# GpSimd's weight and condition splits in 256-column instructions, and the first down-weight split moved ahead of a wait

## What is computed

```python
h = _gcn(h, src, dst, gcn_in_w, gcn_in_b, n)
for i in range(L):                                   # L = 4
    a = _attn(_ln(h, ln2_w[i], ln2_b[i]), cond, Wq[i], Wk[i], Wv[i], Wo[i])
    h = h + a
    u = _ln(h, ln3_w[i], ln3_b[i]) @ geglu_w[i] + geglu_b[i]
    val, gate = jnp.split(u, 2, axis=-1)
    f = val * jax.nn.gelu(gate, approximate=False)
    h = h + f @ ffo_w[i] + ffo_b[i]
h = _gcn(h, src, dst, gcn_out_w, gcn_out_b, n)
```

## Time and profile before

| | us |
|---|---|
| median of 3 runs | 2378.5 (2378.1 to 2378.63) |
| the profiled execution, whole | 2377.68 |
| its span in the trace | 2375.9 |
| TensorE busy | 2315.6 |
| VectorE busy | 1658.8 |
| ScalarE busy | 1243.8 |
| GpSimd busy | 1038.9 |

### The profile page before, as it was taken

The page is one execution under the profiler, slowest core; times in us unless marked ns, Lnnn a source line. Parts: engine busy times, 40 slices in busy tenths (PEclk is TensorE's granted clock), DMA queues, the critical chain, the costliest instruction groups (busy, mean ns, idle before and its releaser), DMA issues.

```text
span 2375.9 us, 38716 instructions
## 1 busy us (share of the span) xinstructions
PE 2315.6 (97%) x14414; PEld 2043.8 (86%) x14414; DVE 1658.8 (70%) x3053; ACT 1243.8 (52%) x2585; POOL 1038.9 (44%) x696
## 2 busy tenths in 40 slices
PE   7899999999999999999999999999999999999999
PEld 5358999988888999988888999988888999988887
DVE  9976776786657676786657666786667667785554
ACT  9955767654434555653434555644434655643322
POOL 3025877566653322266652322266652322265530
PEclk9999999999999999999999999999999999999999
DMA  2033333212232333212232333222232433122230
GB/s 80 1 132 135 146 148 152 98 49 67 62 120 79 118 106 106 82 54 62 63 120 80 123 107 106 74 60 61 61 117 81 125 116 108 63 63 62 62 125 36
DMA packets 115882, 214.57 MB, mean 90 GB/s; under 512 B 9520, under 2 KB 71600, under 8 KB 113904
## 3 DMA queue, kind: packets, MB, share of 16 engines
q1 hardware_dynamic: 115408, 207.89, 26.6%
q10 hardware_dynamic: 288, 4.19, 0.4%
HBM read 176.13 MB, written 35.91 MB: 89 GB/s over the span
## 4 chain that ended last, share of the span: by engine, by line
PE 84%; DVE 9%; POOL 2%; ACT 2%; issue 2%; DMA 0%; DVEq 0%; SPq 0%; ACTq 0%; POOLq 0%
PE ps L2367 9%; PE ps L2368 9%; PE ps L2369 9%; PE ps L2616 9%; PE ps L2619 8%; PE ps L2618 8%; PE ps L2741 7%; PE ps L2743 7%; PE ps L2745 7%; PE ps L2644 2%; PE ps L2666 2%; PE ps L2668 2%; DVE oh_d L1683 1%; PE ps L2943 1%; PE ps L2663 1%
## 5 line engine op out<-in xcount | busy, mean ns | idle before, releaser
L2616 PE MATMUL ps<-cb,wk_hi 128*128 128x256 f32 x896 | 258.3, 288 | 4.6 <-POOL cb L803 3.6
L2616 PE MATMUL ps<-wv_hi,cb 128*128 128x256 f32 x896 | 257.4, 287 | 4.6 <-DVE kv L1985 4.4
L2618 PE MATMUL ps<-cb,wk_hi 128*128 128x256 f32 x896 | 253.7, 283 | 0.0
L2619 PE MATMUL ps<-cb,wk_lo 128*128 128x256 f32 x896 | 253.7, 283 | 0.0
L2619 PE MATMUL ps<-wv_hi,cb 128*128 128x256 f32 x896 | 253.7, 283 | 0.0
L2618 PE MATMUL ps<-wv_lo,cb 128*128 128x256 f32 x896 | 253.7, 283 | 0.0
L864 POOL TENSOR_TENSOR f_lo<-ff,f_hi 128x512 fp32r<-128x512 f32 x128 | 168.7, 1329 | 172.0 <-ACT f_hi L1484 171.9
L823 POOL TENSOR_TENSOR v_lo<-kv,v_hi 128x512 fp32r<-128x512 f32 x96 | 124.4, 1296 | 260.2 <-ACT v_hi L1238 260.1
L2302 DVE TENSOR_TENSOR h<-h,ps 128x512 f32<-128x512 f32 x256 | 169.3, 684 | 65.4 <-PE ps L2369 64.8
L2368 PE MATMUL ps<-wf_lo,f_hi 128*128 128x512 f32 x512 | 199.3, 389 | 0.0
L2367 PE MATMUL ps<-wf_hi,f_hi 128*128 128x512 f32 x512 | 199.3, 389 | 0.0
(11 more groups left out here) (377 smaller groups left out, 6892.0 us busy)
## 6 DMA issues: line engine op xcount, KB each, us to landing
cb<-cb_s SPq DMA_DIRECT2D x168, 512.0 KB, 4.6
stage<-in_pieces SPq DMA_DIRECT2D x256, 128.0 KB, 2.6
cb_s<-cb SPq DMA_DIRECT2D x56, 512.0 KB, 2.6
stage<-in_pieces SPq DMA_DIRECT2D x44, 512.0 KB, 3.7
stage<-in_condT SPq DMA_DIRECT2D x7, 1024.0 KB, 5.8
stage<-in_pieces SPq DMA_DIRECT2D x16, 256.0 KB, 3.3
at_s<-at_hi ACTq DMA_DIRECT2D x2, 2048.0 KB, 11.8
wo_raw<-in_pieces SPq DMA_DIRECT2D x8, 512.0 KB, 4.4
```

Source lines behind the costliest of these rows:

```text
L2616: pe.matmul(to, l_hi, r_hi, start=(fresh and i == 0 and k == 0), stop=False, skip_group_check=True)
L2618: pe.matmul(to, l_hi, r_lo, start=False, stop=False, skip_group_check=True)
L2619: last = pe.matmul(to, l_lo, r_hi, start=False, stop=(k == 1), skip_group_check=True)
```

## The change

Each subtraction of GpSimd in `w_low`, `attn_low`, `cond_sum`, `cond_low` and `set_low` becomes instructions of 256 columns each: 4 for 1024, 3 for 768, 2 for 512. The semaphore is raised by the last of them. `kv_low`, `f_low`, `wq_low` and `wo_low` stay whole. And `down_low(0)` stands ahead of the wait for `x3_ok`.

```diff
@@ w_low
-                pool.tensor_tensor(lo, stage[:, slot, :], bits(hi), ALU.subtract).then_inc(w_ok, 1)
+                for c in range(0, 768, 256):
+                    pool.tensor_tensor(lo[:, c:c + 256], stage[:, slot, c:c + 256], bits(hi[:, c:c + 256]), ALU.subtract)
+                pool.tensor_tensor(lo[:, 768:1024], stage[:, slot, 768:1024], bits(hi[:, 768:1024]), ALU.subtract)\
+                    .then_inc(w_ok, 1)
@@ cond_sum
-                pool.tensor_tensor(out, a, b, ALU.subtract).then_inc(c_sum, 1)
+                pool.tensor_tensor(out[:, 0], a[:, 0], b[:, 0], ALU.subtract)
+                pool.tensor_tensor(out[:, 1], a[:, 1], b[:, 1], ALU.subtract).then_inc(c_sum, 1)
@@ cond_low
-                pool.tensor_tensor(cb[:, j, 1], cond_source(g, j), bits(cb[:, j, 0]), ALU.subtract).then_inc(c_lo, 1)
+                hi, lo, source = bits(cb[:, j, 0]), cb[:, j, 1], cond_source(g, j)
+                pool.tensor_tensor(lo[:, 0], source[:, 0], hi[:, 0], ALU.subtract)
+                pool.tensor_tensor(lo[:, 1], source[:, 1], hi[:, 1], ALU.subtract).then_inc(c_lo, 1)
@@ set_low (attn_low alike)
-                    pool.tensor_tensor(lo[:, 0:3, :], stage[:, r % 2, 256:1024].rearrange("p (b n) -> p b n", n=256),
-                                       bits(hi[:, 0:3, :]), ALU.subtract)
+                    for b in range(3):
+                        pool.tensor_tensor(lo[:, b, :], stage[:, r % 2, 256 * b + 256:256 * b + 512],
+                                           bits(hi[:, b, :]), ALU.subtract)
                     pool.wait_ge(w_hi_ok, FIRST_PIECES + PIECES * l + r + 1)
...
-                        pool.tensor_tensor(lo[:, 3:7, :], sums_s[:, :, :], bits(hi[:, 3:7, :]),
+                        for b in range(3):
+                            pool.tensor_tensor(lo[:, 3 + b, :], sums_s[:, b, :], bits(hi[:, 3 + b, :]), ALU.subtract)
+                        pool.tensor_tensor(lo[:, 6, :], sums_s[:, 3, :], bits(hi[:, 6, :]),
                                            ALU.subtract).then_inc(w_ok, 1)
@@ between attention and feed-forward
+                down_low(0)
                 wait_apart(pool, x3_ok, 2 + NT * l + NT)
-                down_low(0)
                 set_low(1, 0)
```

More of the change, by code:

```diff
@@ L779, in attn_low @@
                 pool.wait_ge(w_hi_ok, n + 1)
-                pool.tensor_tensor(lo[:, 0:3, :], stage[:, n % 2, 256:1024].rearrange("p (b n) -> p b n", n=256),
-                                   bits(hi[:, 0:3, :]), ALU.subtract)
-                pool.tensor_tensor(lo[:, 3:7, :], sums_s[:, :, :], bits(hi[:, 3:7, :]), ALU.subtract)\
-                    .then_inc(w_ok, 1)
+                for b in range(3):
+                    pool.tensor_tensor(lo[:, b, :], stage[:, n % 2, 256 * b + 256:256 * b + 512], bits(hi[:, b, :]),
+                                       ALU.subtract)
+                for b in range(3):
+                    pool.tensor_tensor(lo[:, 3 + b, :], sums_s[:, b, :], bits(hi[:, 3 + b, :]), ALU.subtract)
+                pool.tensor_tensor(lo[:, 6, :], sums_s[:, 3, :], bits(hi[:, 6, :]), ALU.subtract).then_inc(w_ok, 1)
             def cond_sum(g, n):
```

## The result

| | before | after |
|---|---|---|
| median of 9 runs, us | 2377.87 (2377.14 to 2378.63) | 2382.72 (2380.44 to 2386.77) |
| the profiled execution, whole | 2377.68 | 2380.44 |
| its span in the trace | 2375.9 | 2378.6 |

The ratio is 1.0021, with a 95% interval from 1.0012 to 1.003. The forecast was 2380.7: 2.2 us more than the 2378.5 that stood for the kernel before, where the measurement beside the changed kernel has it at 2377.87 and the difference at 4.85. Two numbers of this table do not fit each other: the profiled execution is 2.8 us slower than before, the median 4.9. And while the nine runs of before lie within 1.5 us, those of after lie 6.3 us apart. Both have one cause, which the forecast did not have.

What follows compares the result with a forecast made beforehand. TensorE, busy 97% of the span, bounds the kernel, so only its waits count. Opening 0.4, layer 0 start 1.05, first groups 1.0, other groups 0.8, borders -1.0 give +2.2 us: median 2380.7, range 2374.9 to 2384.5.

Steps and rivals of the forecast that it cites:

- What a cut costs: On GpSimd, 256-column pieces start 0.69 us apart, so cutting into 2, 3 or 4 costs 0.13, 0.26 or 0.40 us.
- The opening, +0.4: One cut of 1024 columns delays x_veps, for which VectorE waits with nothing else to do: +0.4 us.
- The start of layer 0, +1.05: Cuts ahead of GpSimd's norm delay p_exp, for which TensorE waits; the condition's second block is swallowed there: +1.05 us.
- The first groups, +1.0: First condition groups: cuts delay the value split by 1.7 us, of which VectorE gives back about 0.9; taken as +1.0.
- the condition's chain: Rival at the condition: VectorE gives nothing back, two more cuts show per later group; +4.6 to +5.6 us; chance 0.13.
- The other groups, +0.8: Six later condition groups: one cut block of 512 columns delays TensorE by 0.13 us in each, +0.8 us in all.
- The border: Between attention and feed-forward, four times: the first set's wait goes, set (1, 1)'s grows to 2.8 us; -0.25 us each.
- The rule of taking turns: GpSimd and VectorE: the later instruction waits out the whole earlier one, then needs some 0.13 us less than alone.
- VectorE does not get in between the pieces: Rival at the border: set (1, 1) takes 4.9 us, each border brings -1.7, sum -3.6 us, 2374.9; chance 0.08.
- a piece costs only its columns: Rival on GpSimd: a piece costs 0.55 us, cuts are free in layer 0, sum about -7 us, 2371.5; chance 0.06.
- the move buys nothing: Rival at the border: the last tile's chain loses what set (1, 0) gains; +7.8 us, 2386.3; chance 0.04.
- GpSimd's busy time: Sign in the profile after, over the whole kernel: GpSimd's busy time up by some 30 to 50 us.

Runs made afterwards that it cites:

- the kernel with the filled wait: The changed kernel plus 11 useless TensorE products of 512 columns ahead of its wait for the low parts of set (1, 1): 2379.7 us.
- the cuts alone: The changed kernel with down_low(0) back behind the wait for x3_ok, all cuts kept: 2387.51 us.
- the condition's cuts: The kernel before with down_low(0) moved ahead of its wait, and only cond_sum and cond_low cut into instructions of 256 columns: 2378.0 us.
- the attention weights' cuts: The kernel before with down_low(0) moved ahead of its wait, and only attn_low cut into seven instructions of 256 columns: 2378.0 us.
- the move alone: The kernel before with down_low(0) ahead of GpSimd's wait for x3_ok, no instruction cut: 2376.14 us.
- half filled: The changed kernel plus 5 useless TensorE products, instead of 11, ahead of its wait for set (1, 1): 2379.65 us.
- the fastest one: The kernel before with w_low and set_low cut, down_low(0) moved, attention and condition whole, and set (1, 1) made earlier: 2366.41 us.

## Why the prediction was right and where it was wrong

The time came out 2.0 us above the forecast and inside its range. The change itself cost 4.85 us where +2.2 was forecast; the two come nearer as times because the forecast started from a median of before that was 0.6 us higher. The parts, one by one:

- **What a cut costs** (0.69 start to start): right. In GpSimd's free-running stretches most pieces start 0.69 to 0.71 apart.
- **The opening, +0.4:** not told apart. VectorE's wait for x_veps went from 0.69 to 0.94 us, but the mark that TensorE passes at 150.3 us in this execution lies between 150.5 and 151.4 in all other profiles, with the cut and without. On the two chips where both kinds ran it is 150.9 to 151.4 with the cut and 150.8 to 151.1 without, so the 0.4 may be there; it can't be told from what else moves.
- **The start of layer 0, +1.05:** +1.07, but not in the wait that I named. I had the condition's second block swallowed by the wait for p_exp, which would grow to 2.3. TensorE asks for that block before, and had next to no slack for it; its wait for p_exp stayed at 1.24:

```profile
180.48 0.39 PE L2627 MATMUL ps<-cb,wk_hi 128*128 128x256 f32 x1 [0.91 <-POOL cb L811]
183.41 0.33 PE L2695 MATMUL ps<-ident,o_full 128*128 128x128 f32 x1 [1.24 <-DVE p_exp L1948]
```

- **The first groups, +1.0:** mis-sized, +1.61, which is the first half of the rival called the condition's chain. The full 1.7 of the cuts arrived, less 0.1. I had VectorE give back 0.9 behind 252.75, and it did: TensorE's wait of 1.01 there is gone. But GpSimd, which has no pause here, then made the next wait longer by 0.74, and TensorE's waits of the whole stretch sum up to 4.9 us instead of 3.2:

```profile
229.26 0.39 PE L2627 MATMUL ps<-wv_hi,cb 128*128 128x256 f32 x1 [1.92 <-DVE kv L1996]
...
276.58 0.39 PE L2627 MATMUL ps<-cb,wk_hi 128*128 128x256 f32 x1 [1.22 <-POOL cb L811]
```

  Before, the chain that ends in this last wait ran through TensorE's own products up to 269.65. Now it runs through GpSimd's sums, condition blocks and value splits from 254.3 to 268.9: a gain on one engine is none where the other one has become the later.
- **The other groups, +0.8:** for the five behind that wait +0.13 each, 0.65, as worked out (0.48 to 0.61 us). The span shows +0.37, since one of the five groups took 0.28 us longer before. The second half of that rival, two more cuts in each group, did not come.
- **The border:** -0.4 each instead of -0.25, and nearly every step at its time. GpSimd and VectorE in layer 1, where TensorE starts the attention's last step 3.87 us later than before:

```profile
1020.17 2.32 POOL L733 TENSOR_TENSOR wf_lo<-stage,wf_hi 128x256 fp32r<-128x256 f32 x3
1022.45 1.46 POOL L734 TENSOR_TENSOR wf_lo<-stage,wf_hi 128x256 fp32r<-128x256 f32 x1
1025.51 4.14 POOL L899 TENSOR_TENSOR wg_lo<-stage,wg_hi 128x256 fp32r<-128x256 f32 x3 [1.59 <-DVE xT_lo L2102]
1029.61 0.92 POOL L903 TENSOR_TENSOR wg_lo<-stage,wg_hi 128x256 fp32r<-128x256 f32 x1
...
1038.60 2.52 POOL L899 TENSOR_TENSOR wg_lo<-stage,wg_hi 128x256 fp32r<-128x256 f32 x3 [0.36 <-DVE sums_s L2266]
1041.08 3.27 POOL L907 TENSOR_TENSOR wg_lo<-sums_s,wg_hi 128x256 fp32r<-128x256 f32 x3
1044.30 0.72 POOL L908 TENSOR_TENSOR wg_lo<-sums_s,wg_hi 128x256 fp32r<-128x256 f32 x1
```

```profile
1020.24 0.96 DVE L2089 TENSOR_SCALAR z<-h,mv,rstd 128x512 f32<-128x512 f32 x1 [0.44 <-POOL rstd L727]
...
1039.10 2.29 DVE L2243 TENSOR_TENSOR w_lo<-z,w_hi 128x256 fp32r<-128x256 f32 x3
```

```profile
1045.08 0.50 PE L2752 MATMUL ps<-xT_hi,wg_hi 128*128 128x512 f32 x1 [2.77 <-POOL wg_lo L908]
```

  Less 3.87: the down weights start at 1016.30 (forecast 1016.3), set (1, 0) ends at 1026.66 (1026.6), set (1, 1) starts at 1034.73 (1034.7) and ends at 1041.15 (1041.1). Its seven pieces take 6.42 us (6.4), TensorE waits 2.77 (2.8), and the norm of the last tile takes 0.96 (1.0). The rule of taking turns carries all of it. One step of that working was 0.2 short: by its own terms TensorE ends the full product at 1041.26 - 1.73 - 0.95 - 0.1 = 1038.5 and not at 1038.3; it was 1038.44. That VectorE does not get in between the pieces, and that a piece costs only its columns, the two rivals on the faster side, are out. So is the one that the move buys nothing: without it the kernel is 5.1 us slower.
- **The step that failed** is the one at the end of the border: "TensorE waits from 1038.3 on, 2.8 us instead of 1.73. Of the 0.95 gained, 0.15 is left". It counts the wait at its length. The two waits of 1.1 and 1.7 us became one of 2.8, and behind that one the clock falls in some executions. Without the clock the sum comes near: the kernel with the filled wait is 2.2 us above before on its chip, and the sum was +2.2. That they are equal is partly luck. In the stretches of the first profile, without the fall, the change costs 1.3 us, because the later groups (0.4 for 0.8) and the borders (-1.6 for -1.0) gave more than the first groups took (1.6 for 1.0), and the opening can't be told. The clock is the other 2.6 us of the median, and what spreads the executions. What would have shown the danger was in sight: I wrote down a wait of 2.8 us, where the profile of before has none above 1.8 us outside its opening, and in the opening, where there are longer ones, the granted clock is 0.93 in the mean of the first 150 us.
- **GpSimd's busy time** rose by 88.8 us, not 30 to 50. The 560 more pieces at the forecast's own 0.13 would already be 73, and by durations (4 x 0.72 - 2.39 = 0.49 for three more, so 0.16 each) they are 91, an estimate that leaves nothing for VectorE's turns. None of it shows in the steady feed-forward, as forecast.

## What to carry to other kernels

Cutting an instruction on one of two engines that shut each other out moves time to the engine that was cut, so cut where the other engine's result is needed first, and leave whole where one's own is: here the same cut of the sets cost 9.5 us in one order (some 6 of it in waits, the rest by the clock) and was worth 6.2 in another. A moved step brings in its own instructions as obstacles: whole, the moved step made TensorE wait 1.56 us for the last norm, and in quarters that wait was gone. And two short waits are not always worth one long one: when an edit merges TensorE's waits, look at the granted clock behind the merged wait, over several executions, and whether a later wait takes the loss up.

## What the runs showed of the hardware that I had not expected

- Behind a TensorE wait of 2.77 us the granted clock was 0.50 for some 3 us at one of four places in one execution and in three of four in another, once for longer. It cost 1.4 to 1.6 or 2.8 us where no wait followed. Behind four waits of 3.22 us (the cuts alone) it fell at three places. Behind four waits of 1.65 us, and behind the four of 1.7 before the change, it stayed at 1.00; behind waits of 1.56 us for another result it fell at three of four places in one kernel (the condition's cuts), at two in another (the attention weights' cuts) and at none in a third (the move alone). It did not fall behind the wait of 1.87 to 2.11 us at 230 us, which each of the five kept profiles with both the condition and the attention weights cut has. So the length of the wait alone does not tell; what does is open.
- Products of no use made a kernel faster, by keeping the clock up: by 2.6 us with eleven of them, each kernel against before on its own chip, and by 2.9 with five, on one chip.
- That a kernel's executions lie far apart can itself be a sign of the clock: 6.3 us for the changed kernel, 1.1 with its waits filled, 2.0 with them half filled, 1.3 for the fastest one.
